# A decoder megakernel on one core: expert groups of six and two tiles, fillers placed by planned activity, last bias on VectorE, all queues in a new order

## The chip, the cores and the metric

One core of a Trainium2 chip runs the whole program. The metric is the device time of one execution in microseconds (us). TensorE (PE in the rows) multiplies matrices, VectorE (DVE) and ScalarE (ACT) work on tiles and read PSUM, GpSimd (POOL) does powers, products and indirect transfers, and SyncE (SP) starts the other transfers.

## The reference

The input x is 16 sequences of 64 tokens of 128 features. Six residual steps follow each other: an attention with ternary weights and quantised inputs (called A below), a cross attention to a context (B), a mixture of eight experts with top 2 routing, a linear attention (D), a match of every token against 64 text rows, and a feed-forward with a gridded GELU.

```python
x = x + L0_attn(layernorm(x))             # A
x = x + L0_xattn(ctx, ctx, layernorm(x))  # B
# experts: each token goes to 2 of 8 experts
h = silu(einsum('th,ehf->etf', x, w1)) * einsum('th,ehf->etf', x, w3)
out = einsum('etf,efh,te->th', h, w2, w)
x = x + L1_attn(layernorm(x))             # D
x = x + text[argmax(sim(x, text))]        # match
h = float2fix(pwlin_gelu(float2fix(x @ w1 + b1)))
x = x + float2fix(h @ w2 + b2)            # last
```

## The kernel before

The 1024 tokens are 8 tiles of 128 rows. An attention on one tile is a job, as A3 or D7. A job is a chain of stages over four engines: `stats`, `rstd` (POOL), `front`, `xT`, `xTin` (ACT), `proj`, `take` (ACT), `scores`, `shift` (DVE), for A and B also `maxT`, `qadd`, `again` and `exps` (a second pass of scores less their maximum), then `values`, `norm`, `yT`, `yTin`, `out` and `update`. Stages named `xT`, `proj`, `scores`, `again`, `values`, `yT`, `out` run on TensorE.

The experts work on groups of tiles. When the B jobs of a group are done, each tile is normalised (`pnorm`), its router logits are made (`pT`, `logits`), VectorE picks the two experts (`route`), TensorE counts the places (`rank`), VectorE makes addresses (`slots`, `table`, `home`), and POOL scatters each tile twice to HBM (`scat`, line 624, one indirect DMA of 64 KB each). Then come units of 128 rows of one expert. A group of n tiles has (2n*128 + 8*127)//128 units, whatever the router chose. SP loads weights (`W`, 768 KB, four buffers) and rows (`X`, 64 KB) of a unit and stores its result (`Y`, 64 KB). TensorE turns the rows (`xgT`, line 714), makes two halves `gu` (line 698, 8 recorded matmuls each), and `down` (line 707, 8 recorded matmuls); ACT (`uo`), DVE (`gate`) and POOL (`h`, line 602) work between `gu` and `down`. `W` of unit u waits for `down` of unit u-4. When all units of a group are stored, POOL gathers two rows for each token (`gath`, line 634) and DVE combines them (`comb`). Only then can the D jobs of those tiles start.

The end is four stages p, each for two tiles: `gstats`, `gnorm`, `gT`, `sim`, `best`, `pickT`, `got`, `gadd`, `zpow`, `znorm`, `zT` (the match), then `zh0`/`zh1`, `ha`, `nodes`, `gelu`, `blend`, `zout` (lines 983 and 985) and `finish` (the feed-forward). The stages share the tile `xz`: `gnorm` of p waits for `zT` of p-1.

The order on every engine is fixed when the program is built. `stages()` gives each stage an engine, a cost and what it waits for; `plan()` plays these costs through and takes, at each moment, the ready stage of the greatest urgency (the length of the path behind it plus a number from `URGENCY`). What runs on the chip are only the queues that come out, with semaphore waits. Where the plan has TensorE idle it puts `keep_warm`, one 384-column bf16 matmul into a bank whose contents are dead (line 992), here called a filler.

Of the kernel before, what the change touches and what calls it, by code (L numbers as in the profile page):

```python
# [67 lines left out]
URGENCY = {
    'W': 30, 'X': -10, 'Y': -56, 'add': 8, 'again': -105, 'best': -50, 'bias': -300, 'blend0': -85,
    'blend1': -30, 'clear': -3, 'comb': 30, 'down': -321, 'exps': -292, 'finish': 303, 'front': -33, 'gT': -10,  # L70
    'gTin': 30, 'gadd': -89, 'gains': -83, 'gate': -10, 'gath': -28, 'gelu0': -100, 'gelu1': -22, 'gnorm': 128,
    'got': 123, 'gu': -52, 'h': 94, 'ha0': -308, 'ha1': -300, 'home': -15, 'kept': -33, 'keyd': 30,
    'lgcopy': 312, 'logits': 326, 'maxT': 50, 'mix': -100, 'mults': -100, 'near': 30, 'nexp': -33,
    'nodes0': -10, 'nodes1': 13, 'norm': -6, 'out': 30, 'pT': -262, 'pTin': -264, 'pad': 100, 'params': -12,
    'pickT': -15, 'pickin': 38, 'pnorm': 8, 'projv': 315, 'prstd': 103, 'pstats': 10, 'qadd': 320, 'qkvout': 2,
    'rank': -6, 'rms': -297, 'rotA': 30, 'rotB': 120, 'route': -300, 'scat': -10, 'scores': 10, 'sim': 18,
    'slots': -91, 'stats': -108, 'take': -22, 'tern': -38, 'text': 46, 'textin': -128, 'tk': -103, 'tkin': -30,
    'tn': 77, 'tnT': -10, 'tnin': 97, 'tnorm': -10, 'tnorm2': -30, 'tp0': 30, 'tp1': 10, 'tpin0': -10,
    'tpin1': 10, 'tsum': -30, 'turn': 42, 'tv': 3, 'tvin': -30, 'uo': 7, 'update': -10, 'values': -113,
    'xT': 309, 'xTin': 300, 'xgT': -10, 'xgTin': -183, 'yTin': 2, 'yq': -47, 'ysave': -100, 'zT': 100,  # L80
    'zTin': -80, 'zexp': 22, 'znorm': -100, 'zout': 10, 'zpow': -13,}
# [169 lines left out]
def plan():  # L251
# [34 lines left out]
    while events:  # L286
        now = min(e[0] for e in events)
        for event in sorted(e for e in events if e[0] == now):
            events.remove(event)
            s = event[2]  # L290
            if not s:
                continue
            for filler in empties.get(s, ()):
                for bank in banks(filler):
                    full[bank] -= 1
                    freed[bank] = now
            for f in followers.get(s, ()):
                missing[f] -= 1
                if not missing[f]:
                    ready[st[f][0]].append(f)  # L300
        for e in engines:
# [1 line left out]
            if e == "tensor" and not can and free_at[e] <= now and any(ev[2] for ev in events):
                if now < fill_at:
                    if (fill_at, 1, ()) not in events:
                        events.append((fill_at, 1, ()))
                    continue
                rested = [(freed.get(name, 0.0), k) for k, name in enumerate(SPARE) if not full.get(name)]
                if not rested or min(rested)[0] > now - REST:
                    continue  # L310
                order[e].append(("keep_warm", min(rested)[1]))
                free_at[e] = now + WARM
                fill_at = now + PACE
                events.append((free_at[e], 1, ()))
# [1440 lines left out]
```

How the kernel before makes its waits and increments, by code:

```python
            def clear(_):  # L539
                sp.wait_ge(presets, PRESETS)
                sp.wait_ge(dma_param, 16)
                for g in range(NGRP):
                    sp.dma_start(d["xg"][g].rearrange("(p c r) n -> p c (r n)", p=P, c=2 * max(SIZE)),
                                 zeros[:, :].unsqueeze(1).to_broadcast([P, 2 * max(SIZE), 512])).then_inc(cleared, 16)
# [1 line left out]
            def weights_in(u):  # L547
                g, j = UNIT[u]
                sp.wait_ge(C["tab_ready"], g + 1)
                if u >= WB:
                    sp.wait_ge(C["down_mm"], u - WB + 1)
                row = sp.value_load(tab[g][0:1, 0, j:j + 1], min_val=0, max_val=(E - 1) * P)
                sp.dma_start(wbuf[:, u % WB, :], d["w"][bass.ds(row, P), :]).then_inc(w_loaded[u % WB], 16)
# [1 line left out]
            def rows_in(u):  # L555
                g, j = UNIT[u]
                sp.wait_ge(C["tab_ready"], g + 1)
                sp.wait_ge(scattered[g], 16 * 2 * SIZE[g])
                if u >= WB:
                    sp.wait_ge(C["xgT_mm"], u - WB + 1)
                row = sp.value_load(tab[g][0:1, 1, j:j + 1], min_val=0, max_val=E * REGION - P)
                sp.dma_start(xg[:, u % WB, :], d["xg"][g][bass.ds(row, P), :]).then_inc(xg_loaded[u % WB], 16)
# [1 line left out]
            def rows_out(u):  # L564
                g, j = UNIT[u]
                sp.wait_ge(C["y_saved"], u + 1)
                sp.dma_start(d["yg"][g][j * P:j * P + P, :], ys[:, u % WB, :]).then_inc(y_stored[u % WB], 16)
```

## Time and profile before

| | before |
|---|---|
| median of 3 runs | 376.45 us (375.62 to 376.56) |
| the profiled execution | 373.39 us |
| its span, first to last instruction | 371.8 us |
| TensorE busy | 331.7 us, 89% |
| VectorE, ScalarE, GpSimd busy | 236.8, 160.6, 140.3 us |
| mean granted TensorE clock | 0.945 |
| moved by DMA | 38.51 MB, mean 104 GB/s |
| fillers | 275 of 4923 recorded matmuls |

A share is an average over very different stretches: attention with hardly a transfer, experts with the DMA engines near full, and an end of short dependent steps. So the time has to be read by stretch. PEclk is the granted clock in parts of 2.4 GHz; 0.5 is the lower level, 1.2 GHz. A matmul's recorded time is a latency, so matmuls in a row are timed by the distance of their starts.

### The profile page before, as it was taken

Reading aid. Unit: us, or ns where it says so; the run is one execution under the profiler, and the core shown is the slowest. Engines: PE = TensorE matmul, PEld = TensorE weight load, DVE = VectorE, ACT = ScalarE, POOL = GpSimd, SP = SyncE. Lnnn points to the kernel's source line nnn. Section 1 sums busy time; section 2 is a strip of 40 time slices with the busy share of each in tenths; the row PEclk is TensorE's granted clock in tenths of the full one; section 3 lists DMA queues with packets and bytes.
Section 4 is the critical chain, followed back from the end, with each engine's and each line's share of the span. In section 5 each row is a group of like instructions: output and inputs, shape, how many; then the busy total and the mean of one; then the engine's idle time right before and its main releaser. Section 6 shows DMA issues by size and latency. Waiting matters only on the chain.

```text
span 371.8 us, 12672 instructions
## 1 busy us (share of the span) xinstructions
PE 331.7 (89%) x4923; PEld 262.3 (71%) x4923; DVE 236.8 (64%) x774; ACT 160.6 (43%) x466; POOL 140.3 (38%) x173
## 2 busy tenths in 40 slices
PE   0788999999999999999989888999996899977857
PEld 0335766877776778899788877999984679754535
DVE  4787755658778755256862126756679676887781
ACT  1475463523542135344545454744455065605040
POOL 5069511114283615033694367722352730110000
PEclk9999999969989889999999999999999699989895
DMA  8760000000000923605978799644300100000000
GB/s 273 281 260 2 4 2 4 4 2 4 3 4 18 330 100 103 206 9 168 294 212 255 237 307 302 218 135 158 100 15 16 53 13 5 2 0 17 0 15 14
DMA packets 19724, 38.51 MB, mean 104 GB/s; under 512 B 2129, under 2 KB 13009, under 8 KB 19538
## 3 DMA queue, kind: packets, MB, share of 16 engines
q1 hardware_dynamic: 17458, 34.62, 28.7%
q0 software_dynamic: 1024, 2.10, 1.7%
q10 hardware_dynamic: 1184, 0.99, 0.8%
q8 instruction: 39, 0.64, 0.7%
q14 instruction: 19, 0.16, 0.1%
HBM read 29.98 MB, written 7.73 MB: 101 GB/s over the span
## 4 chain that ended last, share of the span: by engine, by line
PE 63%; issue 8%; DMA 7%; DVE 6%; POOL 4%; ACT 2%; SPq 2%; POOLq 0%; ACTq 0%
PE Op L879 12%; PE FU L698 7%; PE FU L820 5%; PE Sp L806 4%; PE FU L992 4%; PE Mp L983 3%; PE AC L707 2%; PE Qp L752 2%; PE Sp L820 2%; POOL hh L602 2%; DMA yr<-yg,home 2%; PE Mp L849 2%; DMA wbuf<-in_w 1%; PE Sp L992 1%; DMA yg<-ys 1%
## 5 line engine op out<-in xcount | busy, mean ns | idle before, releaser
L596 POOL TENSOR_TENSOR rstd<-powed,minus_half 128x1 f32<-128x1 f32 (+1 forms) x36 | 22.4, 622 | 120.2 <-DVE powed L1208 94.3
L698 PE MATMUL FU<-xgT,wbuf 128*128 128x128 f32 x480 | 62.1, 277 | 4.3 <-DMA wbuf<-in_w 3.5
L698 PEld LDWEIGHTS FU<-xgT,wbuf 128*128 128x128 f32 x480 | 57.8, 192 | 7.6 <-DMA wbuf<-in_w 5.3
L602 POOL TENSOR_TENSOR hh<-hh,uu 128x256 f32<-128x256 f32 x60 | 43.2, 730 | 44.8 <-DVE hh L1533 41.3
L1533 DVE SCALAR_TENSOR_TENSOR hh<-th,FU 128x256 f32<-128x256 f32 x60 | 24.7, 420 | 37.4 <-ACT uu L1009 33.9
L1019 ACT ACTIVATE th<-FU 128x256 f32<-128x256 f32 x60 | 23.1, 385 | 44.6 <-PE FU L698 43.9
L992 PE MATMUL FU<-causal_b,identb 128*128 128x384 bf16 x149 | 36.5, 362 | 0.0
L707 PE MATMUL AC<-wbuf,hh 128*128 128x128 f32 x240 | 31.9, 276 | 2.0 <-POOL hh L602 2.0
L596 POOL TENSOR_TENSOR rms<-rms,minus_half 128x20 f32<-128x20 f32 x8 | 28.5, 3570 | 11.3 <-DVE rms L1303 11.3
L707 PEld LDWEIGHTS AC<-wbuf,hh 128*128 128x128 f32 x240 | 29.3, 192 | 2.8 <-issue 2.6
L1093 ACT ACTIVATE pT<-FU 128x1024 f32<-128x1024 f32 x16 | 16.5, 1031 | 33.9 <-PE FU L820 33.9
L1374 DVE TENSOR_REDUCE mpad<-Sp 128x8 f32<-128x512 f32 x32 | 20.6, 687 | 11.1 <-PE Sp L806 11.1
L1009 ACT ACTIVATE uu<-FU 128x256 f32<-128x256 f32 x60 | 22.9, 381 | 0.0
L983 PE MATMUL Mp<-params,hq 128*128 128x128 f32 x64 | 12.7, 361 | 9.5 <-DVE hq L1574 6.9
L992 PEld LDWEIGHTS FU<-causal_b,identb 128*128 128x128 bf16 x149 | 15.6, 108 | 7.3 <-issue 2.1
L992 PE MATMUL Sp<-causal_b,identb 128*128 128x384 bf16 x80 | 20.0, 349 | 0.0
L634 POOL DMA_INDIRECT yr<-yg,home x16 | 15.8, 985 | 11.1 <-DMA yg<-ys 8.0
L624 POOL DMA_INDIRECT xg<-xall,slot x16 | 15.9, 997 | 9.9 <-DVE slot L1461 6.2
L983 PEld LDWEIGHTS Mp<-params,hq 128*128 128x128 f32 x64 | 10.9, 257 | 11.9 <-issue 11.7
L879 PEld LDWEIGHTS Op<-vtok,pT 64*64 64x64 f32 x512 | 15.7, 135 | 2.6 <-issue 1.5
L879 PEld LDWEIGHTS Op<-textv,pT 64*64 64x64 f32 x512 | 16.1, 138 | 1.7 <-issue 0.7
L879 PE MATMUL Op<-vtok,pT 64*64 64x9 f32 x512 | 16.2, 200 | 0.8 <-issue 0.6
(264 smaller groups left out, 696.6 us busy)
## 6 DMA issues: line engine op xcount, KB each, us to landing
wbuf<-in_w SPq DMA_DIRECT2D x30, 768.0 KB
xg<-zeros SPq DMA_DIRECT2D x2, 2048.0 KB, 10.3
xg<-xg SPq DMA_DIRECT2D x30, 64.0 KB, 3.3
yg<-ys SPq DMA_DIRECT2D x30, 64.0 KB, 4.4
params<-in_params SPq DMA_DIRECT2D x1, 1632.5 KB, 10.8
x<-in_x ACTq DMA_DIRECT2D x1, 512.0 KB, 4.9
text<-in_ctx SPq DMA_DIRECT2D x1, 512.0 KB, 7.4
out<-x SPq DMA_DIRECT2D x4, 128.0 KB, 1.8
```

Of the source, the lines that this page charges most:

```text
L596: return nc.gpsimd.tensor_tensor(o, base, exponent[:, 0:o.shape[1]], ALU.pow)
L602: nc.gpsimd.tensor_tensor(hh[:, u % NB, :], hh[:, u % NB, :], uu[:, u % NB, :], ALU.mult)\
L698: ins = mm(FU[:, v % 2, 256 * part + P * i:256 * part + P * i + P], wbuf[:, u % WB, c:c + P], xgT[:, u % 2, :], start=True, stop=True)
L707: ins = mm(AC[:, 0:P], hh[:, (2 * u + i // 2) % NB, P * (i % 2):P * (i % 2) + P], wbuf[:, u % WB, c:c + P], start=i == 0, stop=i == FC - 1)
L820: ins = mm(bank[o, r, at:at + 64], key(n, c)[rows, e, o], qT[rows, b, c, o], start=first, stop=True, skip_group_check=not first)
L879: ins = mm(Op[c, w * h:w * h + w], pT[c, b, h, :], v, start=True, stop=True)
L983: ins = mm(Mp[:, P * i:P * i + P], hq[:, c, P * i:P * i + P], f_w2[:, c, :], start=(c == 0), stop=False)
L992: mm(bank, identb[:, :], causal_b[:, :].unsqueeze(1).to_broadcast([P, 6, 64]), start=True, stop=True)
L1009: return nc.scalar.activation(o, i, ACT.Copy)
L1019: nc.scalar.activation(th[:, u % NB, :], FU[:, u % 2, 0:256], ACT.Tanh, scale=0.5)
L1374: ins = v.tensor_reduce(at[:, :, r, :], sc[:, 8 * r:8 * r + 8, :].rearrange("p (c e) k -> p c e k", c=2), X, ALU.max)
L1533: v.scalar_tensor_tensor(hh[:, u % NB, :], th[:, u % NB, :], 1.0, FU[:, u % 2, 0:256], ALU.add, ALU.mult)\
```

## The change

`SIZE` goes from (4, 4) to (6, 2): the first group holds tiles 0 to 5 and has 19 units instead of 15, the second holds tiles 6 and 7 and has 11. Units 0 to 29 stay 30 in all. Group 0 makes 12 scatters and 12 gathers, group 1 makes 4 and 4. The zeroed HBM area grows from 2 x 2048 KB to 2 x 3072 KB. In the last step, the bias is no longer a matmul of one row (16 recorded matmuls in all); VectorE adds it in `finish`. The planner places fillers in a pass of its own, after the order is made, only where the planned activity of TensorE in the time just before is low. `JOBS` and `URGENCY` get other numbers, and so all queues another order. TensorE's fillers fall from 275 to 212: 51 before `out` of tile 5's B job, 48 more before the first `xgT`, 6 up to the first `down`, then none before the last `down` (unit 29), and 107 behind it. Before, they were 112 up to the end of the last B job, 37 up to the last `down`, and 126 behind.

```diff
-SIZE = (4, 4)
+SIZE = (6, 2)
 JOBS = [(j[0], int(j[1])) for j in (
-    "A0 A1 A2 A4 A3 B0 B1 B2 B3 A7 B4 A5 A6 B7 B5 B6 D0 D1 D2 D3 D4 D5 D7 D6").split()]
+    "A1 A0 A2 A4 A3 B0 B1 B2 A5 B3 B4 A7 A6 B5 B6 B7 D0 D1 D2 D4 D3 D5 D7 D6").split()]
 URGENCY = {
-    'W': 30, 'X': -10, 'Y': -56, 'add': 8, 'again': -105, 'best': -50, 'bias': -300, 'blend0': -85,
+    'W': -289, 'X': -38, 'Y': 105, 'add': 30, 'again': -83, 'best': -47, 'bias': -315, 'blend0': -50,
...
-PACE = 0.42
 REST = 1.5
+SPAN, LIVELY = 3.41, 0.48
...
-        add("zout", p, "tensor", 2.1, [("blend0", p), ("blend1", p)], "Mp", [("finish", p)])
-        add("finish", p, "vector", 0.9, [("zout", p)])
+        add("zout", p, "tensor", 1.8, [("blend0", p), ("blend1", p)], "Mp", [("finish", p)])
+        add("finish", p, "vector", 1.24, [("zout", p)])
...
+def with_fillers(stages_in_order, begun, st, vacant):
+
+    row, past, at = [], [], START["tensor"]
+    for s in stages_in_order:
+        while at + WARM <= begun[s]:
+            past = [(t, c, a) for t, c, a in past if t + c > at - SPAN]
+            lively = sum(a * (t + c - max(t, at - SPAN)) / c for t, c, a in past)
+            rested = [(f, SPARE.index(name)) for name, spells in vacant.items() for f, e in spells if f <= at - REST and e >= at + WARM]
+            if lively > LIVELY * SPAN or not rested:
+                at += 0.1
+                continue
+            row.append(("keep_warm", min(rested)[1]))
+            past.append((at, WARM, 0.16))
+            at += WARM
+        row.append(s)
+        past.append((begun[s], st[s][1], ACTIVITY.get(s[0], 0.0)))
+        at = begun[s] + st[s][1]
+    return row
...
                         ins = mm(Mp[:, P * i:P * i + P], hq[:, c, P * i:P * i + P], f_w2[:, c, :],
-                                 start=(c == 0), stop=False)
-                    ins = mm(Mp[:, P * i:P * i + P], ones[0:1, :], f_b2[0:1, :], start=False, stop=True)
+                                 start=(c == 0), stop=(c == FC - 1))
...
-                link(v.tensor_scalar(fo[:, :], Mp[:, 0:256], GRID256, GRID256, ALU.add, ALU.subtract))
+                link(v.tensor_tensor(fo[:, :].rearrange("p (t n) -> p t n", t=2), Mp[:, 0:256].rearrange("p (t n) -> p t n", t=2),
+                                     f_b2.unsqueeze(1).to_broadcast([P, 2, D]), ALU.add))
+                link(v.tensor_scalar(fo[:, :], fo[:, :], GRID256, GRID256, ALU.add, ALU.subtract))
```

TensorE's queue around the first expert unit, before (L714 is `xgT`, L698 `gu`; L752, L806 and L891 belong to attention jobs, L992 are fillers):

```order
L752 MATMUL Qp<-xnT,params 128x128 x2
L714 MATMUL Mp<-consts,xg 128x128
L992 MATMUL Sp<-causal_b,identb 128x384 x3
L806 MATMUL Sp<-keyT,qT 64x256 x8
L714 MATMUL Mp<-consts,xg 128x128
L698 MATMUL FU<-xgT,wbuf 128x128 x4
L891 MATMUL AC<-consts,yint 128x128
```

The same place of the changed program (L733 is `xgT`, L717 `gu`, L726 `down`, L1010 the fillers, L740 to L745 `rank` of group 1; L924 is the last B job's `out`, L931 and L950 `pT` and `logits` of tiles 6 and 7):

```order
L924 MATMUL AC<-params,yT 128x128
L1010 MATMUL Qp<-causal_b,identb 128x384 x10
L931 MATMUL Qp<-consts,xall 128x128 x2
L950 MATMUL Mp<-params,xallT 128x8 x2
L1010 MATMUL Sp<-causal_b,identb 128x384 x11
L733 MATMUL Mp<-consts,xg 128x128
L1010 MATMUL Sp<-causal_b,identb 128x384
L740 MATMUL Mp<-hot_b,before_b 128x16
L742 MATMUL Mp<-hot_b,ones_b 128x8
L745 MATMUL Mp<-hot_b,ones_b 128x8 x2
L717 MATMUL FU<-xgT,wbuf 128x128 x8
```

All A and B jobs now stand ahead of the first unit; before, four of the sixteen jobs were unfinished there, and their work stood between the first units. From the first `down` to `gu` 52 the changed queue is `gu`, `gu`, `down`, `xgT` over and over, with nothing else.

POOL's queue between the B jobs and the units, before (L624 scatters, L596 powers, L602 is `h`):

```order
L624 DMA xg<-xall,slot 4096x128 x8
L596 TENSOR_TENSOR rstd<-powed,minus_half 128x1
L615 TENSOR_TENSOR x<-x,params 128x128
L596 TENSOR_TENSOR rstd<-powed,minus_half 128x1
L615 TENSOR_TENSOR x<-x,params 128x128
L602 TENSOR_TENSOR hh<-hh,uu 128x256 x2
```

and in the changed program (L643 scatters, L615 powers, L621 is `h`):

```order
L643 DMA xg<-xall,slot 6144x128 x12
L615 TENSOR_TENSOR rstd<-powed,minus_half 128x2
L643 DMA xg<-xall,slot 6144x128 x4
L621 TENSOR_TENSOR hh<-hh,uu 128x256 x43
L653 DMA yr<-yg,home 128x128
```

The first `h` now stands behind twelve scatters of group 0 and behind all four of group 1; before, behind eight of group 0 alone.

TensorE's queue behind the last `down`, before (the last row shown is `pickT` of p = 1; `gT` of p = 0 was long done):

```order
L912 MATMUL Qp<-consts,xz 128x128 x2
L707 MATMUL AC<-wbuf,hh 128x128 x4
L946 MATMUL Mp<-tnormT,xzT 64x64 x4
L992 MATMUL Sp<-causal_b,identb 128x384 x9
L912 MATMUL Qp<-consts,pick 128x128 x2
```

and in the changed program, where `gT` of p = 0 follows the last `down`, and work of D2, D4, D3 and D5 stands behind it:

```order
L726 MATMUL AC<-wbuf,hh 128x128 x4
L931 MATMUL Qp<-consts,xz 128x128 x2
L924 MATMUL Op<-params,yT 128x128
L779 MATMUL Mp<-xnT,params 128x128
L780 MATMUL Mp<-params,xnT 128x144
L771 MATMUL Qp<-xnT,params 128x128 x2
L773 MATMUL Qp<-xnT,params 128x128
L898 MATMUL Op<-vn,pT 64x8 x32
```

So all four stages p lie behind the last unit now, where before the first was past its match, and only two D jobs wait for the last gathers instead of four.

## Rows read from the trace of the kernel before

**Rows 1.** The page: busy time, share, instructions of each engine.

```profile
PE 331.7 (89%) x4923; PEld 262.3 (71%) x4923; DVE 236.8 (64%) x774; ACT 160.6 (43%) x466; POOL 140.3 (38%) x173
```

**Rows 2.** Windows: stretch, its length, busy (count) per engine, PEclk, DMA share, GB/s.

```profile
0.00:167.06 167.06, 152.71 (x2791) 111.02 (x2792) 107.74 (x411) 71.14 (x195) 63.23 (x70) 0.95 0.26 89
167.06:281.05 113.99, 105.33 (x1286) 97.78 (x1287) 64.22 (x193) 57.49 (x196) 59.93 (x81) 1.00 0.62 196
281.05:338.29 57.24, 50.15 (x732) 38.29 (x733) 44.07 (x127) 23.67 (x59) 16.48 (x22) 0.91 0.06 17
338.29:371.80 33.51, 23.49 (x120) 15.20 (x118) 20.81 (x46) 8.34 (x17) 0.69 (x1) 0.80 0.03 9
```

**Rows 3.** Windows of line 992 alone, the fillers: PE and PEld.

```profile
0.00:167.06 167.06, 29.02 (x112) 12.17 (x112) 0.95 0.26 89
167.06:281.05 113.99, 9.72 (x37) 3.87 (x37) 1.00 0.62 196
```

**Rows 4.** Timeline of PE, jobs and first units: start, us, what.

```profile
115.09 0.18 PE L721 MATMUL Mp<-hot_b,before_b 128*128 128x32 bf16 x1
...
133.89 0.48 PE L714 MATMUL Mp<-consts,xg 128*128 128x128 f32 x1
...
141.41 1.06 PE L707 MATMUL AC<-wbuf,hh 128*128 128x128 f32 x8
...
147.79 1.09 PE L806 MATMUL Sp<-keyT,qT 64*64 64x256 f32 x16
...
149.19 1.16 PE L820 MATMUL FU<-qT,keyT 64*64 64x64 f32 x64
...
156.67 2.04 PE L879 MATMUL Op<-textv,pT 64*64 64x9 f32 x64
158.64 0.49 PE L905 MATMUL AC<-params,yT 128*128 128x128 f32 x2
```

**Rows 5.** Timeline of DVE: B3's update, then first and last of route.

```profile
100.77 0.29 DVE L1419 TENSOR_TENSOR x<-x,AC 128x128 f32<-128x128 f32 x1 [0.20 <-PE AC L905]
...
111.14 0.18 DVE L1431 TENSOR_REDUCE thr<-base 128x4 f32<-128x32 f32 x1
...
113.59 0.19 DVE L1449 TENSOR_TENSOR hot_b<-hot 128x32 bf16<-128x32 f32 x1
```

**Rows 6.** Timeline of POOL: first and last of eight scatters.

```profile
116.78 1.18 POOL L624 DMA_INDIRECT xg<-xall,slot  x1 [5.38 <-DVE slot L1461]
...
125.94 0.96 POOL L624 DMA_INDIRECT xg<-xall,slot  x1 [0.30 <-issue]
```

**Rows 7.** Timeline of SP: a W, then (left out) X and Y, the next W.

```profile
211.87 0.34 SPq L553 DMA_DIRECT2D wbuf<-in_w  x1
...
214.67 0.34 SPq L553 DMA_DIRECT2D wbuf<-in_w  x1
```

**Rows 8.** Timeline of PE: two downs of one unit's distance.

```profile
193.44 1.06 PE L707 MATMUL AC<-wbuf,hh 128*128 128x128 f32 x8
...
196.23 1.06 PE L707 MATMUL AC<-wbuf,hh 128*128 128x128 f32 x8
```

**Rows 9.** Windows as above: eight units, four W alone, jobs at the lower clock.

```profile
201.09:231.57 30.48, 25.74 (x212) 23.94 (x213) 9.59 (x27) 14.66 (x50) 17.39 (x23) 1.00 0.87 278
128.00:131.00 3.00, 2.83 (x76) 2.24 (x69) 1.87 (x9) 1.28 (x4) 0.42 (x1) 0.74 1.01 414
73.70:82.20 8.50, 8.50 (x157) 6.90 (x157) 3.81 (x18) 2.20 (x5) 1.47 (x3) 0.60 0.01 2
```

**Rows 10.** Timeline of PE: zT of p = 2 and 3, last fillers, last bias.

```profile
335.16 0.44 PE L912 MATMUL Qp<-consts,xz 128*128 128x128 f32 x2
...
351.67 0.38 PE L912 MATMUL Qp<-consts,xz 128*128 128x128 f32 x2
...
354.58 3.58 PE L992 MATMUL FU<-causal_b,identb 128*128 128x384 bf16 x21
...
367.64 0.79 PE L985 MATMUL Mp<-params,ones 1*128 1x128 f32 x2
```

More of the change, by code:

```diff
@@ L72 @@
[L72 to L76, printed above, removed]
@@ new lines @@
+    'blend1': -50, 'clear': -300, 'comb': -18, 'down': -309, 'exps': -10, 'finish': 4, 'front': -48, 'gT': 30,
+    'gTin': -105, 'gadd': 80, 'gains': 300, 'gate': 300, 'gath': -100, 'gelu0': 3, 'gnorm': -30, 'got': 369,
+    'gpow': -300, 'gstats': -100, 'gu': -100, 'h': 331, 'ha0': -8, 'ha1': -31, 'home': 109, 'kept': 30,
+    'keyd': -30, 'lgcopy': 24, 'logits': -39, 'maxT': 128, 'mix': -100, 'mults': -300, 'near': -20,
+    'nexp': -300, 'nodes0': 30, 'nodes1': 122, 'norm': 7, 'out': 323, 'pT': 10, 'pTin': -10, 'pad': 100,
@@ new lines @@
+    'params': 27, 'pickT': -100, 'projv': 308, 'prstd': -108, 'pstats': -11, 'qadd': 92, 'qkvout': 300,
+    'rank': 10, 'rms': -38, 'rotA': 10, 'rotB': 13, 'rotM': -100, 'route': -100, 'rstd': -10, 'scat': 30,
+    'scores': 73, 'shift': 10, 'sim': 33, 'slots': -280, 'stats': -102, 'table': 297, 'take': 100, 'tern': -52,
+    'text': 21, 'tk': -52, 'tn': -30, 'tnT': -131, 'tnin': -280, 'tnorm': -10, 'tnorm2': 100, 'tp0': 30,
+    'tp1': 10, 'tpin0': -10, 'tpin1': 10, 'tsum': -300, 'turn': 337, 'tv': -78, 'tvin': -300, 'uo': -41,
@@ L82 @@
+    'update': 7, 'values': -65, 'xT': 280, 'xTin': -10, 'xgT': 26, 'xgTin': 22, 'yT': 10, 'yTin': 58, 'yq': 305,
+    'ysave': -348, 'zT': -10, 'zTin': 2, 'zexp': 20, 'zh0': -50, 'zh1': 260, 'znorm': 141, 'zout': -300,
+    'zpow': 128,}
 LANDING = {'scat': 3.0, 'gath': 2.8, 'W': 5.0, 'X': 2.6, 'Y': 4.2}
@@ L85 @@
 WARM = 0.18
-PACE = 0.42
 REST = 1.5
+SPAN, LIVELY = 3.41, 0.48
+ACTIVITY = {
+    "xT": 0.11, "turn": 0.32, "projv": 0.45, "maxT": 0.21, "values": 0.12, "yT": 0.11, "tk": 0.85, "tv": 0.43, "text": 0.21,
+    "tnT": 0.21, "pT": 0.21, "logits": 0.03, "xgT": 0.11, "gu": 0.85, "down": 0.85, "gT": 0.21, "sim": 0.21, "pickT": 0.21,
+    "got": 0.43, "zT": 0.21, "zh0": 0.85, "zh1": 0.85, "zout": 1.7, "scores": 0.9, "again": 0.95, "proj": 0.35, "out": 0.16}
 SPARE = ("FU0", "FU1", "AC", "Qp", "Mp", "Op", "Sp")
@@ L275, in plan @@
     free_at = dict(START)
-    full, freed, empties, fill_at, table = {}, {}, {}, 0.0, 0
+    full, empties, table, begun = {}, {}, 0, {}
+    vacant = {name: [[0.0, 1e9]] for name in SPARE}
     waiting = set(turn_of.values()) | set(turn_of)
@@ L295, in plan @@
                     full[bank] -= 1
-                    freed[bank] = now
+                    if not full[bank] and bank in vacant:
+                        vacant[bank].append([now, 1e9])
             for f in followers.get(s, ()):
@@ L302, in plan @@
             can = [s for s in ready[e] if not any(full.get(k) for k in banks(s)) and turn_of.get(s) not in waiting] if free_at[e] <= now else []
[L303 to L314, printed above, removed]
             if can:
```

11 lines of the change are left out of this document (4 added, 7 removed).

## The prediction

> **What bounds the kernel now.** The page comes first: TensorE is busy 89% of the span, no other engine over 64% [rows 1]. That is not yet a bound, since 275 of its matmuls are fillers. So the next view is the table of windows, cut where the work changes [rows 2], and the same windows for the fillers' line [rows 3]. Up to the end of the last B job (167.06 us), TensorE is busy 152.7 us with 112 fillers in it. A filler in a row takes 0.163 us: 21 of them start at 354.58 and end 3.58 us later, less one latency of 0.33 [rows 10]. So the fillers are 18.3 us there, and TensorE, or what feeds it, is the bound: it has almost no idle time after the first 30 us, and where a filler stands it either fills a wait or delays real work by its length. From 167.06 to 281.05 us (last `down`) TensorE is busy 105.3 of 114.0 with 37 fillers, at DMA share 0.62: units and four D jobs, a dense stretch. In the last 90.75 us (the third and fourth of [rows 2]) TensorE is busy with fillers, the real chain runs through VectorE (64.9 busy) and short steps on all engines. The reader should see three regimes: TensorE-bound attention, units paced by TensorE, SP and weights together, and a serial end.
>
> **The change, stretch by stretch.** I cut the changed program at the same kinds of places and work out each length.
>
> *Start to `out` of B5 (job 13).* Before takes 167.06 to finish all B jobs. Off come 112 fillers (18.3) and the expert work inside: 14 blocks of `gu` or `down` and 7 `xgT`. One unit is 2.79 us from `down` to `down` when nothing waits [rows 8], so a block is 0.89 and an `xgT` 0.11: 13.3 in all. Off also comes what now lies behind `out` of B5, two B jobs and two router steps. A B job is scores 1.09, again 1.16, values 2.04, out 0.49 [rows 4] and about 0.9 for its small matmuls: 5.7, so 12.0. On come the 51 fillers that stay: 8.3. That is 131.8 if no wait shows up where the other 61 fillers (9.9) stood. If all of it does, 141.7. Since the queue is reordered to have other work there, I take a fifth: +2.0, so **133.8**. The clock I leave as it was.
>
> *`out` of B5 to `rank` of group 0.* All six tiles must be routed before anything of an expert starts. The chain is update, normalisation, `pT`, logits, `route` (2.65 from 111.14 to 113.78, [rows 5]), and ahead of the logits copy on VectorE stand B6's front and shift, which wait for its projection and scores: with 0.3 to 0.4 for each small step and 1.1 and 1.3 for scores and shift I get 8.6. Before, B3's update to `rank` was 14.3 (100.77 to 115.09, [rows 4, 5]), with TensorE full of other jobs; that is the upper end. **8.6.**
>
> *`rank` to the end of the first `down`.* Before: 115.09 to 141.41 + 0.9 = 27.2, hidden under attention jobs [rows 4]. Scatters follow each other at 1.26 us ((125.94 - 116.78)/7 = 1.31 with a slow first, [rows 6]); four more cost 5.0. Then POOL's order matters: the first `h` is behind group 1's four scatters, which need `rank` of group 1, and that stands behind the first `xgT` on TensorE. `xgT` comes at 18.8 + 5.0 + 0.8 (slots now wait for a shift) = 24.6 after `rank`; then rank and slots of group 1 (1.7), four scatters (5.0), two `h` (1.6), `down` (1.0): **33.9**. What hides it: remaining TensorE work there is two halves of B jobs and four `gu`, about 13 us. So some 20 us of TensorE are bare now that before were covered. This is the price of the grouping. `W` is queued early and has no part in it.
>
> *First `down` to `gu` 52.* Unit after unit with nothing between. TensorE's floor is 2.79 [rows 8]. SP's floor is 2.80: W, X and Y, and the next W at 211.87 and 214.67 [rows 7]. The transfers: a unit moves 0.917 MB, and eight units with their gathers had 278 GB/s at share 0.87 [rows 9], so 320 GB/s at full share and 2.87 us a unit. These eight units took 30.48 us, 3.81 each [rows 9], but with waits of SP out of step and gathers between. Three floors of 2.8 to 2.9 beside each other do not add up to 2.87; I take 3.05, nearest to the floors because the new SP queue repeats W, Y, X regularly. The first two units run on loaded weights (6.1), then 22 units: 6.1 + 22 x 3.05 = **73.2**. Bounds: 2.79 gives 67.5, 3.81 gives 89.9.
>
> The Trainium skill (DMA: Bandwidth & Descriptors, § Specifications) gives about 358 GB/s as the HBM limit of a core. By it a unit would be 2.56 us, under TensorE's 2.79, and this stretch 67.5 instead of 73.2. The rows do not bear the figure out either way: with four W alone in flight 414 GB/s moved [rows 9], with X, Y and gathers among them 278 at share 0.87. I go by the rows.
>
> *`gu` 52 to the last `down`.* 8 `gu`, 6 `down`, 2 `xgT`: 12.7. Beside them stand 3.6 D jobs. Before, the like stretch is `gu` 44, where [rows 9] end (231.57), to the last `down` at 281.05: 49.5 us, with 25 blocks and 6 `xgT` of units in it (23.0), a match of about 4 and some fillers, so four D jobs took about 22, or 5.5 each. 12.7 + 3.6 x 5.5 = **32.7**.
>
> *Last `down` to the end.* Before: 90.75 us [rows 2]. Now `gT` of p = 0 starts right there, and through `xz` the four stages p form one chain. Up to `gT` of p = 3, before needed 57.24, with VectorE busy 44.1. Now VectorE has there: 44.1, plus match of p = 0 and start of p = 1 (6.4), plus remainders of D4, D3, D5 (7.7), less two D jobs that are done (9.0), plus the longer `finish` (0.9) = 50. It is 88% full, and I find the same 57 when I walk its new order. Behind it, before took 33.51; the bias matmuls go (2 x 0.72 of the last p at this clock, [rows 10]), one blend moves out of the way of `gadd` (1.2 of it helps), the new add costs 0.45: 31.3. **88.3.** The cover of the bias matmuls in p = 0 to 2 is VectorE's own work, so they gain nothing there.
>
> Sum: 133.8 + 8.6 + 33.9 + 73.2 + 32.7 + 88.3 = **370.5**, against 371.8 before, 1.3 less. The profiled execution was 373.39 in time, the median of the runs shown is 376.45; I take the difference off the median: about **375**.
>
> The zeroing of HBM grows by 2 MB. It runs in the first 50 us beside nothing that waits for it, since scatters start after 100 us: 0. `rank` has 12 matmuls instead of 8, under 0.1.
>
> **The rivals.** A measurement of this kernel can tell a change from about 0.3%, 1.1 us.
>
> *Dense units at TensorE's floor and attention that closes up.* 2.79 instead of 3.05 saves 5.7, no returned waits 2.0: 367. For it: the floors of SP and TensorE are equal and nothing else is in the queues. Against: the eight units of [rows 9].
>
> *The last stretch is shorter.* Only two D tiles remain behind the last gathers. If the walk through VectorE overstates and the chain through `xz` alone counts (13.4 a match, from 338.29 to 351.67, and 3.1 to the next `gT`, from 335.16 to 338.29 [rows 2, 10], three times, and 31.3), it is 81, and the whole about 368. Against: VectorE is nearly full.
>
> *Weights fall behind: slower.* W of a unit waits for `down` four units before, in a dense row that is twice the unit's time for issue and landing. If one more transfer in flight makes it land later, the pace is 3.4 to 3.81, and the stretch 7.7 to 16.7 longer: 383 to 392. It decides at 3.16 a unit, where the gain of 1.3 and 1.1 more are eaten. The eight units of [rows 9] speak for it.
>
> *The filler time comes back: slower.* All 9.9 us become waits, or the clock falls more often because TensorE has fewer fillers: +8, 383. The clock fell before in 73.7 to 82.2 us to a mean of 0.60 with TensorE busy 8.50 of 8.50 us and fillers in the row [rows 9], so idle time alone is not what does it, and fillers did not prevent it. The Trainium skill (TensorE: Matmul & The Clock Gate, § Why this matters for your kernels) ties the fall to idle gaps between bursts; by that the bare 20 us before the units would start them at 1.2 GHz and, lasting as in [rows 9], cost some 4 us, while the closed-up attention would be safe. The row contradicts it for the attention.
>
> *The change does nothing.* If all gains and prices cancel, 376.
>
> **How the numbers follow.** The forecast as worked out, 371 to 379, 0.42. Units at the floor or closed-up attention 0.18, shorter end 0.15, weights behind 0.13, fillers' time back 0.12. Of the forecast's own 0.42, 0.19 lie under 375.3, 0.10 within 0.3%, 0.13 above. Faster: 0.19 + 0.18 + 0.15 = 0.52; same 0.10; slower 0.13 + 0.25 = 0.38. For 8 in 10 the range goes to 364 below (both gains together) and 384 above.
>
> **What would show it.** The first `xgT` at about 167 us and a hole before it with TensorE on fillers and idle; the first `h` behind the sixteenth scatter; `down` to `down` 3.0 to 3.1 us for some 22 units, with short waits on wbuf; last `down` at 282; the end 88 long with VectorE over 80% busy up to `gT` of p = 3. Wrong would be: `out` of B5 outside 128 to 140, a unit's pace outside 2.9 to 3.2, an end under 84.

## The result and the profile after

The changed kernel took 380.39 us in the median of 8 runs (378.15 to 383.98), the kernel before 376.38 (375.13 to 378.47): a ratio of 1.0133, 95% interval 1.009 to 1.0177. Medians, here and below, are over all runs; ratios and their intervals leave out runs over 1.5% above the fastest of the same kernel. The changed kernel is slower by 1.3%; forecast was about 375, slightly faster. The profiled execution took 380.45 us with a span of 378.8, against the 370.5 of the sum. Its table of busy times, to be set beside [rows 1]:

```profile
PE 323.1 (85%) x4844; PEld 258.9 (68%) x4844; DVE 233.2 (62%) x778; ACT 161.9 (43%) x466; POOL 140.7 (37%) x173
```

TensorE is 8.6 us less busy and the span is 7 us longer, so the loss is idle time and slower matmuls, not more work. The windows, cut at the places of the prediction's sum (end of B5's `out`, end of the first `down`, end of the last, `gT` of p = 3), as [rows 2]:

```profile
0.00:138.06 138.06, 120.80 (x2293) 85.69 (x2293) 87.98 (x333) 59.00 (x153) 46.20 (x49) 0.92 0.21 72
138.06:180.80 42.74, 32.41 (x436) 23.14 (x436) 27.55 (x121) 8.77 (x25) 20.04 (x23) 0.91 0.33 113
180.80:287.30 106.50, 101.09 (x1214) 97.68 (x1213) 47.07 (x130) 60.90 (x211) 60.30 (x83) 0.98 0.72 233
287.30:345.65 58.35, 49.59 (x799) 38.54 (x798) 49.25 (x149) 24.85 (x62) 13.09 (x17) 0.97 0.04 12
345.65:378.80 33.15, 19.17 (x108) 13.89 (x107) 21.33 (x48) 8.41 (x17) 1.11 (x1) 0.89 0.03 9
```

| term of the sum | forecast | measured | |
|---|---|---|---|
| start to `out` of B5 | 133.8 | 138.1 | +4.3 |
| to `rank` of group 0 | 8.6 | 10.5 | +1.9 |
| to the end of the first `down` | 33.9 | 32.3 | -1.6 |
| to `gu` 52 | 73.2 | 74.5 | +1.3 |
| to the end of the last `down` | 32.7 | 32.0 | -0.7 |
| to the end | 88.3 | 91.5 | +3.2 |

The first window's clock is 0.92, where the kernel before had 0.95 over its own first window [rows 2]. Three stretches up to `rank` of group 0 have a low clock, while TensorE is busy nearly all the time:

```profile
78.00:88.50 10.50, 10.50 (x170) 8.37 (x167) 5.87 (x26) 4.09 (x10) 3.71 (x7) 0.52 0.01 3
103.00:108.50 5.50, 5.37 (x130) 5.08 (x133) 3.46 (x15) 1.72 (x7) 4.51 (x3) 0.70 0.01 3
128.90:144.50 15.60, 14.31 (x115) 9.56 (x115) 7.08 (x30) 2.77 (x9) 2.65 (x5) 0.56 0.01 2
```

By the clocks of these rows the lower level (0.5) held for some 27 us of the first 148.5; by that of [rows 2], for some 17 of the first 167 before. Both are estimates: twice what the clock lacks to 1, times the length.

The bare hole, on TensorE's timeline (L740 `rank`, L1010 fillers, L931 `pT`, L733 `xgT`, L726 `down`):

```profile
148.52 0.20 PE L740 MATMUL Mp<-hot_b,before_b 128*128 128x48 bf16 x1 [0.81 <-DVE qT L1400]
...
162.57 2.12 PE L1010 MATMUL Qp<-causal_b,identb 128*128 128x384 bf16 x10
167.47 0.44 PE L931 MATMUL Qp<-consts,xall 128*128 128x128 f32 x2 [2.78 <-DVE xall L1229]
...
170.70 0.27 PE L733 MATMUL Mp<-consts,xg 128*128 128x128 f32 x1
...
179.77 1.13 PE L726 MATMUL AC<-wbuf,hh 128*128 128x128 f32 x8 [1.13 <-POOL hh L621]
```

Of the 23 distances from `down` to `down` in the dense units, 17 are 2.78 to 3.01 us, five lie between 3.46 and 4.01 and one is 5.36. The one long wait for a W costs 1.90 us itself and about as much again by the lower clock behind it: two distances of 5.36 and 4.01 us where two of 2.79 would be 3.8 less:

```profile
226.65 2.50 PE L717 MATMUL FU<-xgT,wbuf 128*128 128x128 f32 x16 [1.90 <-DMA wbuf<-in_w]
228.94 1.91 PE L726 MATMUL AC<-wbuf,hh 128*128 128x128 f32 x8
```

At the end (L1002 `zout`, L931 `zT`), `zout` of p = 2 and 3 each stand on the path after an idle wait and run at the lower clock; those of p = 0 and 1, at the upper, take 1.95 and 2.02 us. In the trace of before, `zout` of p = 2 is at the upper clock (348.36 us) and the last at the lower, as here. VectorE writes the second half of `xz` for `zT` of p = 3 by 357.50, and `zT` starts at 360.07 since it is queued behind `zout` of p = 2. VectorE's row, then TensorE's:

```profile
356.90 0.60 DVE L1229 TENSOR_SCALAR xz<-x,mv,rstd 128x128 f32<-128x128 f32 x2
```

```profile
357.13 3.15 PE L1002 MATMUL Mp<-params,hq 128*128 128x128 f32 x16 [2.65 <-DVE hq L1592]
360.07 0.63 PE L931 MATMUL Qp<-consts,xz 128*128 128x128 f32 x2
...
371.60 3.58 PE L1002 MATMUL Mp<-params,hq 128*128 128x128 f32 x16 [4.79 <-DVE hq L1592]
```

### The profile page after: what moved, and what is told of

Its sections match the earlier page's. It is cut to its first block, busy times and chain, and to the rows that moved or that the text cites. A ratio compares the mean times of both kernels' runs of the same rounds, so it can differ in the third digit from the quotient of the medians.

```text
span 378.8 us, 12522 instructions
## 1 busy us (share of the span) xinstructions
PE 323.1 (85%) x4844; PEld 258.9 (68%) x4844; DVE 233.2 (62%) x778; ACT 161.9 (43%) x466; POOL 140.7 (37%) x173
## 4 chain that ended last, share of the span: by engine, by line
PE 24%; DVE 14%; DMA 7%; issue 5%; SPq 2%; POOL 2%; ACT 1%; DVEq 0%; POOLq 0%; ACTq 0%
PE FU L717 7%; DMA wbuf<-in_w 5%; PE AC L726 4%; PE Op L898 3%; PE Mp L1002 2%; PE Sp L839 2%; DVE keyT L1590 2%; DVE keyT L1591 1%; DMA yr<-yg,home 1%; DVE keyT L1589 1%; DMA yg<-ys 1%; PE Qp L991 1%; DVE pT L1384 1%; DVE keyT L1578 1%; DVE stats L1220 1%
## 5 line engine op out<-in xcount | busy, mean ns | idle before, releaser
L717 PE MATMUL FU<-xgT,wbuf 128*128 128x128 f32 x480 | 61.4, 280 | 4.1 <-DMA wbuf<-in_w 3.3
L615 POOL TENSOR_TENSOR rstd<-powed,minus_half 128x1 f32<-128x1 f32 (+1 forms) x36 | 22.3, 620 | 107.4 <-DVE powed L1226 97.9
L717 PEld LDWEIGHTS FU<-xgT,wbuf 128*128 128x128 f32 x480 | 57.2, 194 | 6.1 <-DMA wbuf<-in_w 4.6
L621 POOL TENSOR_TENSOR hh<-hh,uu 128x256 f32<-128x256 f32 x60 | 43.3, 729 | 36.0 <-DVE hh L1551 35.9
L615 POOL TENSOR_TENSOR rms<-rms,minus_half 128x20 f32<-128x20 f32 x8 | 28.3, 3541 | 23.6 <-DVE rms L1321 23.6
L1037 ACT ACTIVATE th<-FU 128x256 f32<-128x256 f32 x60 | 23.0, 383 | 30.7 <-PE FU L717 30.5
L726 PE MATMUL AC<-wbuf,hh 128*128 128x128 f32 x240 | 32.8, 281 | 2.5 <-POOL hh L621 2.5
L726 PEld LDWEIGHTS AC<-wbuf,hh 128*128 128x128 f32 x240 | 30.1, 197 | 2.9 <-issue 2.9
L1010 PE MATMUL FU<-causal_b,identb 128*128 128x384 bf16 x146 | 30.8, 341 | 0.0
L1111 ACT ACTIVATE pT<-FU 128x1024 f32<-128x1024 f32 x16 | 16.4, 1023 | 26.4 <-PE FU L839 26.3
L643 POOL DMA_INDIRECT xg<-xall,slot x16 | 15.6, 976 | 21.1 <-DVE slot L1479 16.8
L898 PEld LDWEIGHTS Op<-textv,pT 64*64 64x64 f32 x512 | 18.7, 157 | 4.2 <-issue 3.7
L898 PE MATMUL Op<-textv,pT 64*64 64x9 f32 x512 | 19.4, 214 | 2.1 <-issue 1.9
L1010 PEld LDWEIGHTS FU<-causal_b,identb 128*128 128x128 bf16 x146 | 14.9, 104 | 7.4 <-issue 1.2
L1002 PE MATMUL Mp<-params,hq 128*128 128x128 f32 x64 | 10.7, 337 | 8.2 <-DVE hq L1592 8.2
L898 PEld LDWEIGHTS Op<-vn,pT 64*64 64x64 f32 x512 | 15.8, 137 | 2.3 <-DVE x L1437 1.4
L898 PE MATMUL Op<-vn,pT 64*64 64x8 f32 x512 | 16.5, 201 | 0.7 <-DVE x L1437 0.7
L898 PE MATMUL Op<-vtok,pT 64*64 64x9 f32 x512 | 16.4, 201 | 0.5 <-issue 0.4
## 6 DMA issues: line engine op xcount, KB each, us to landing
params<-in_params SPq DMA_DIRECT2D x1, 1632.5 KB, 10.5
```

The costliest lines, as they stand in the source:

```text
L615: return nc.gpsimd.tensor_tensor(o, base, exponent[:, 0:o.shape[1]], ALU.pow)
L621: nc.gpsimd.tensor_tensor(hh[:, u % NB, :], hh[:, u % NB, :], uu[:, u % NB, :], ALU.mult)\
L717: ins = mm(FU[:, v % 2, 256 * part + P * i:256 * part + P * i + P], wbuf[:, u % WB, c:c + P], xgT[:, u % 2, :], start=True, stop=True)
L726: ins = mm(AC[:, 0:P], hh[:, (2 * u + i // 2) % NB, P * (i % 2):P * (i % 2) + P], wbuf[:, u % WB, c:c + P], start=i == 0, stop=i == FC - 1)
L898: ins = mm(Op[c, w * h:w * h + w], pT[c, b, h, :], v, start=True, stop=True)
L1010: mm(bank, identb[:, :], causal_b[:, :].unsqueeze(1).to_broadcast([P, 6, 64]), start=True, stop=True)
```

## The experiments

Two theories. **Order:** the loss is the bare hole of the grouping and the later end. **Clock:** fewer fillers, elsewhere, let TensorE's clock fall. The runs were made in five groups, each on a chip of its own: `b_bias`, `b_both`, `a_paced`, `a_none`; `a_again`, `a_wlate`, `b_wlate`, `a_split`; `a_ref`, `a_half`, `a_more`, `bb_split`; `a_scatlate`, `a_more_split`, `bb_more`; `a_ref2`, `a_scatlate2`, `bb_more2`. The kernel before had medians of 378 to 387 there, and 376 beside the result; ratios are to before on the same chip, clocks are means over a kernel's runs. A name with a is an edit of the changed kernel, with b or bb one of the kernel before.

**One part alone in the kernel before.** Bias on VectorE with all queues as they were (`b_bias`); with the new filler pass besides (`b_both`).

```diff
-                                 start=(c == 0), stop=False)
-                    ins = mm(Mp[:, P * i:P * i + P], ones[0:1, :], f_b2[0:1, :], start=False, stop=True)
+                                 start=(c == 0), stop=(c == FC - 1))
...
+    real = [s for s in order["tensor"] if s in st]
+    order["tensor"] = with_fillers(real, begun, st, vacant)
```

> The kernel before with one edit: the bias of the last step is added by VectorE, all queues as before. My theory (the bias counts only in the last of the four stages): 2 x 0.72 us of one-row matmuls go, 0.45 us of VectorE comes, 1.0 us less than before, about 375.4. Rival (the gain is hidden or eaten by VectorE in the first three stages): 376.4 to 377.

> The kernel before with the bias on VectorE and the new filler pass, the order of the real work on all queues as before: 190 fillers instead of 275 (80 instead of 108 ahead of the first down, 3 instead of 41 up to the last, 107 instead of 126 behind). Theory 1 (the change lost by its grouping and order, fillers are neutral): within 1 us of the run with the bias alone, about 375. Theory 2 (fewer fillers cost clock or stand in the wrong places): 3 to 4 us more than the bias alone, 378 to 379, with a mean granted clock below 0.94.

`b_bias`: 376.61 against 384.92, ratio 0.980 (0.972 to 0.988), clock 0.949 against 0.934. `b_both`: 387.74, ratio 1.009 (1.002 to 1.017), clock 0.923. So the new filler pass alone, with 190 fillers instead of 275, took 11 us and 0.026 of the clock: theory 2 of `b_both`, three times as large. Where it loses, one profile of each tells. It reaches `rank` of group 0 at 113.9 us, `b_bias` at 113.8, both at clock 0.97 up to there; to the first `down` it loses 3.9 us, and 7.9 more from the first `down` to the last (`b_bias` first):

```profile
146.84:286.02 139.18, 130.10 (x1806) 119.52 (x1805) 75.34 (x221) 68.35 (x228) 67.08 (x91) 1.00 0.57 181
150.78:297.85 147.07, 131.53 (x1769) 121.88 (x1767) 76.52 (x221) 68.61 (x227) 67.04 (x91) 0.95 0.53 171
```

So the new pass costs clock and time in this order too, but not ahead of `rank`, where the changed kernel lost most.

That the bias gives 8 us and not 1 is explained in part. From the last `down` to the end, the two profiles with the bias matmuls in this order take 91.8 (before) and 92.3 us (`b_wlate`, below), the two without them and with nothing else changed there but fillers 87.9 and 88.3: about 4 us. The last stage p alone is 1.6 shorter than before's (31.96 against the 33.51 of [rows 2]). Where the other 4 us come from stays open.

**Fillers in the changed kernel.** The old rule (`a_paced`), none (`a_none`), a higher limit (`a_more`).

```diff
-    order["tensor"] = with_fillers(order["tensor"], begun, st, vacant)   # a_none
...
-SPAN, LIVELY = 3.41, 0.48
+SPAN, LIVELY = 3.41, 0.75
```

> The changed kernel with the old rule for fillers (one for each 0.42 us of planned idle time): 242 fillers instead of 212, 117 ahead of the first down instead of 105, 19 instead of none up to the last. Theory 1 (fillers neutral): 380, within 1 us of the changed kernel. Theory 2 (the new pass costs clock): 377 to 378 with a granted clock above that of the changed kernel.

> The changed kernel without any filler. Theory 1 (the clock needs them only in the thin stretches): the end doubles its 10.5 us of real matmuls behind gT of p = 3 and about as much before it in part, and the first units start at the lower clock: 388 to 395, mean clock under 0.85. Rival (fillers delay real work as much as they keep the clock): 378 to 382.

> The changed kernel with the limit of planned activity at 0.75 instead of 0.48, so 394 fillers instead of 212: 105 ahead of out of B5 where there are 51 (the kernel before has 110), 194 behind the last down instead of 107. Theory 1 (the attention stretch is late because the clock falls more often without the fillers): granted clock up by 0.02 to 0.04, rank of group 0 at 143 to 146 instead of 148 to 151, the whole 3 to 8 us less. Theory 2 (fillers stand in the way of real work): the clock rises less than the 183 fillers of 0.163 us each cost, 3 to 10 us more.

`a_paced`: 399.26, 1.042 (1.036 to 1.048), on a chip without the changed kernel beside it, so it decides nothing by its time; its profile reaches `rank` of group 0 at 145.0 us, within the spread of the changed kernel's own (below). `a_none`: 419.42 against 384.92, clock 0.818. `a_more`: 395.63, 1.028 (1.021 to 1.035), clock 0.944, beside the changed kernel (`a_ref`) with 407.61, 1.073 (1.054 to 1.092), clock 0.898. 182 more fillers made it 12 us faster. In windows from the start to `rank` of group 0, `a_ref` first, then `a_more`:

```profile
0.00:146.42 146.42, 127.77 (x2352) 89.18 (x2352) 94.64 (x360) 60.93 (x160) 47.73 (x52) 0.92 0.19 68
```

```profile
0.00:140.58 140.58, 128.99 (x2419) 89.59 (x2420) 94.73 (x360) 61.20 (x160) 47.74 (x52) 0.99 0.20 71
```

All 13 profiles with this order lie near one line, about 1 us for 0.01 of clock up to `rank`: 158.1 at 0.85 (`a_none`), 151.2 at 0.89 (`a_split`), 148.5 at 0.91 (the result's), 145.4 at 0.94 (`a_ref2`), 142.2 and 140.6 at 0.99 (`a_more_split`, `a_more`). Nine of them have the very same queue of TensorE up to there, and still spread from 0.89 to 0.94 and from 145.1 to 151.2 us; the two with 54 more fillers ahead of `out` of B5 lie outside that spread, each ahead of the other profiles of this order on its chip (140.6 against 146.4 and 150.2, 142.2 against 149.5).

**The changed kernel again, W later, `zout` in two.** `a_wlate` and `b_wlate` move the second to fourth W behind the first X, since the profiles of the first group had shown TensorE idle by issue behind the four W.

```diff
+        for u in (3, 2, 1):
+            sp_row.remove(("W", u))
+            sp_row.insert(sp_row.index(("X", u)), ("W", u))
```

> The changed kernel itself, once more, beside the kernel before on the chip of this call. The old ratio was 1.013. Theory 1 (the loss is the bare stretch of the grouping and the later end, fixed by the queues): the ratio stays at 1.010 to 1.018. Theory 2 (the size of the loss comes from the clock and from TensorE waiting for instructions while the four first W are in flight, which differ by run and chip): the ratio moves, to under 1.00 or over 1.02, and with it the mean granted clock and the idle time put down to issue.

> The changed kernel as it is, only to have it on the same chip as the other runs of this call. By the two ratios seen so far, 1.013 or 1.054 to the kernel before: near the second where its profile shows TensorE waiting by issue while the twelve scatters of group 0 run, near the first where it doesn't.

> The changed kernel with the second, third and fourth W each moved in SP's queue from ahead of the first X to just ahead of their own X. Theory 1 (nothing but the four transfers keeps TensorE from its instructions there; in the profile with paced fillers 8.2 us of idle time by issue lie in the 20 us after the first W): 5 to 9 us less than the changed kernel wherever that shows such gaps, 0 to 1 where it doesn't, the second unit not later, since its W is issued about 168 us and used about 176. Theory 2 (the gaps have another cause, or the weights now come late for the first units): same or 2 to 6 us more.

> The kernel before with the same edit on SP's queue alone. Theory 1: where before has gaps by issue behind its four W (6.0 us in the profile with the bias alone), they go, but the three later W now run under the jobs and first units that stand right behind, so some come back: 2 to 6 us less. Theory 2: no change, or 2 to 4 us more because W of the second unit is 3 us from its use.

`a_again`: 408.48 against 381.30, ratio 1.054 (1.046 to 1.062), and `a_ref`, shown above, 1.073: on these chips the change costs four to five times as much. What came on top is mostly one stall: of the 22 us by which the profile of `a_again` is longer than the result's, 14.8 lie between `rank` of group 0 and the first `down`, and 4.6 between the last `down` and `gT` of p = 3. TensorE's timeline of `a_ref2`, the same program on a fourth such chip (L898 `values`, L839 `again` of B6 and B7):

```profile
148.05 2.08 PE L898 MATMUL Op<-textv,pT 64*64 64x9 f32 x58 [0.17 <-ACT pT L1111]
150.56 0.26 PE L898 MATMUL Op<-textv,pT 64*64 64x9 f32 x2 [0.43 <-issue]
...
156.34 0.47 PE L839 MATMUL FU<-qT,keyT 64*64 64x64 f32 x2 [0.95 <-issue]
...
162.75 0.26 PE L839 MATMUL FU<-qT,keyT 64*64 64x64 f32 x1 [1.03 <-issue]
...
164.88 1.57 PE L839 MATMUL FU<-qT,keyT 64*64 64x64 f32 x45 [0.44 <-issue]
```

A few matmuls, then half to one microsecond of nothing, for 14 us, with no semaphore in the way. The result's own profile has one gap there, of 1.07 us at 156.90, ahead of the `values` of B7. `a_scatlate2`, below, has 0.79 us at that same place with no scatter near, so this one is no part of the stall. `a_wlate`: 408.23, and 9.2 us of gaps by issue in the 20 us behind its first W, now alone, where `a_again` has 9.7 (the brackets of the timeline's rows summed): so the three later weights are not the cause, and in `a_again` the gaps begin at 154.70, ahead of the first W at 155.43. `b_wlate`: 385.07, ratio 1.007 (1.000 to 1.013); nothing gained there either.

The order of before is not free of the stall. From `rank` of group 0 to the first `down`, it takes 26.3 us in the trace of before and 29.3 in `bb_more`, but 33.0 to 37.1 in its five profiles on the four chips where the changed kernel stalls, a part of it by a lower clock. `b_bias` has three gaps there, 4.33, 0.45 and 1.05 us by issue, from 120.4 to 127.8. So these ratios count only what the stall costs the changed kernel more, and some of what before differs by chip is the stall too.

The cut of `zout` into two parts (`a_split`):

```diff
+                for c0 in (0, 2) if two_parts else (0,):
+                    if c0:
+                        for _ in range(8):
+                            keep_warm(0)
+                        pe.wait_ge(Z["hq_ready"][1], p + 1)
```

> The changed kernel with zout of p = 2 and 3 in two parts: the eight matmuls on the first half of hq as soon as blend0 is done, eight fillers, then the other eight. Theory (zout of p = 2 and 3 stands bare on the path at the lower clock, 3.15 and 3.58 us, and zT of p = 3 waits behind the first of them): 3.0 us less at the lower clock, 4.5 less if the fillers bring it to the upper one. Rival (VectorE is the chain there and takes up what TensorE gives): under 1 us less.

`a_split`: 404.15 beside 408.48, 4.3 less. From `gT` of p = 3 to the end it takes 29.8 us where `a_again` takes 34.4. The edit does two things, since the eight fillers are part of it: `a_more`, with `zout` whole and more fillers, takes 30.7 there, `a_more_split` 29.1. So most of the 4.6 us seems to be the clock, and some 1.6 the cut. Its last `zT` starts 1.0 us behind the start of the second part (L1009), in `a_again` 2.8 behind that of the whole:

```profile
381.44 1.46 PE L1018 MATMUL FU<-causal_b,identb 128*128 128x384 bf16 x8
383.27 1.16 PE L1009 MATMUL Mp<-params,hq 128*128 128x128 f32 x8 [0.36 <-DVE hq L1600]
384.26 0.38 PE L931 MATMUL Qp<-consts,xz 128*128 128x128 f32 x2
```

**Who stalls TensorE.** The twelve scatters run in that very stretch. `a_half` leaves out the second scatter of each tile of group 0, so those rows stay zero, and lets SP wait for six instead of twelve. `a_scatlate`, and again `a_scatlate2`, moves all twelve behind the router's last power.

```diff
+                if g == 0 and k:
+                    return
...
+        at = pool_row.index(("prstd", 3)) + 1
+        pool_row[at:at] = early
```

> The changed kernel with the second scatter of each tile of group 0 left out, so that those rows stay zero: six scatters instead of twelve, nothing else. Theory 1 (TensorE's stall belongs to the scatters: while they run it gets its instructions slowly): the stall ends with the sixth scatter, half as long, and the first unit comes 7.6 us sooner for the missing issues; where the reference shows the stall, the first down comes 8 to 15 us sooner, where it doesn't, 7 to 8. Theory 2 (the stall has nothing to do with the scatters): it stays 13 to 14 us long, and the first down comes 0 to 3 us sooner since TensorE is late anyway.

> The changed kernel with the twelve scatters of group 0 moved in POOL's queue from ahead of the last power of the router (prstd of tiles 6 and 7) to just behind it. So TensorE does the rest of B6 and B7 (again, values, out) before any scatter runs. Theory 1 (the scatters keep TensorE's instructions away): no gaps by issue between rank and the last out, that part takes 12 to 14 us as in the first profile of the changed kernel instead of 27 to 30, power at rank + 15 instead of + 32, first xgT at rank + 33 to 36, so about where it stood (rank + 37): 0 to 4 us less in all. Theory 2 (the gaps belong to this place of TensorE's program, whatever POOL does): the gaps stay, the scatters come behind them, and the first xgT is at rank + 50 or later, 13 us more.

> The changed kernel, one look beside the next kernel. It tells only whether this chip shows the stall: TensorE's last values of B6 start 6 us behind rank without it and 20 us or more with it.

> The changed kernel with the scatters of group 0 behind the router's last power, again. If the look before shows the stall: by theory 1 (the scatters cause it) no gaps by issue here, the router's last power at rank + 15 to 17 and the first xgT at rank + 34 to 37; by theory 2 (the place causes it) gaps as in the look before and the first xgT at rank + 48 or later. If that look shows no stall, nothing is told.

`a_half`: 400.13 beside 407.61; `rank` to the first `down` 37.6 us where `a_ref` has 45.7. POOL's last scatter, and TensorE's last gap:

```profile
159.13 0.96 POOL L645 DMA_INDIRECT xg<-xall,slot  x1 [0.30 <-issue]
```

```profile
161.18 1.99 PE L841 MATMUL FU<-qT,keyT 64*64 64x64 f32 x60 [0.45 <-issue]
```

The stall ends 1.1 us behind the sixth scatter; in `a_ref2` it ends 2.0 behind the twelfth (161.92 + 0.96). From the first gap to the end of the last it lasts 6.3 us, in `a_ref2` 14.8. `a_scatlate` (395.20, 1.044, 1.033 to 1.054) told nothing on this: on its chip `a_more_split`, with the scatters in place, has no stall either. On the chip of `a_ref2`, `a_scatlate2` has its scatters from 165.88 on, and the same two stages before them (L904, L845) run through:

```profile
152.29 2.04 PE L904 MATMUL Op<-textv,pT 64*64 64x9 f32 x64 [0.17 <-ACT pT L1117]
154.26 1.15 PE L1016 MATMUL AC<-causal_b,identb 128*128 128x384 bf16 x6
155.34 1.16 PE L845 MATMUL FU<-qT,keyT 64*64 64x64 f32 x64
...
184.93 0.47 PE L739 MATMUL Mp<-consts,xg 128*128 128x128 f32 x1 [15.16 <-DMA xg<-xg]
...
185.91 3.76 PE L723 MATMUL FU<-xgT,wbuf 128*128 128x128 f32 x16
```

The stall is gone, as theory 1 had it, in one profile of each of the two kernels. The first `xgT` stands at `rank` + 35.3 where `a_ref2` has 36.6, as expected; but TensorE then sat idle for 15 us and does its first two `gu` at the lower clock (3.76 us, 2.02 in the result's timeline at 172.12).

**Both kernels mended.** Bias, split and, in two of them, the limit of 0.75, on the old queues and on the new.

> The kernel before with two edits, the bias on VectorE and zout of p = 2 and 3 in two parts with eight fillers between: a candidate to beat both kernels. The bias alone had 0.980 of before, and in the changed kernel the split took the last stage from gT of p = 3 to the end from 33 or 34 to 29.8 us. Expected 3 to 4 us less than the bias alone, a ratio of 0.970 to 0.975. Rival (VectorE is fuller there in this order): the ratio stays at 0.98.

> The kernel before with the bias on VectorE, zout of p = 2 and 3 in two parts, and the new filler pass with its limit at 0.75: 363 fillers instead of 275 (183 instead of 132 up to the first down, 15 instead of 41 up to the last, 197 instead of 126 behind). If the clock decides, as in the changed kernel where 394 instead of 212 fillers brought it from 0.898 to 0.944 and the time from 406.4 to 394.8: granted clock 0.96 to 0.97 and a ratio of 0.96 to 0.975. If the order before has no idle time left for them, they delay real work: 0.98 to 1.00.

> The changed kernel with the limit at 0.75 and zout of p = 2 and 3 in two parts, 410 fillers in all: with more fillers alone it had 1.028 of before, the split takes another 2 to 4 us off the last 31: ratio 1.015 to 1.025. It does not reach the kernel before where the scatters stall TensorE for 14 us; where they don't, it would be at 0.97 to 0.985.

> The kernel before with the bias on VectorE, zout in two parts and 363 fillers, once more on another chip. It had 0.980 there with the clock at 0.978. Expected 0.965 to 0.985: more gain where the clock of before is lower.

`bb_split`: 378.91, 0.982 (0.972 to 0.992), no more than the bias alone and not the 0.970 to 0.975 expected. `bb_more`: 369.48, 0.980 (0.974 to 0.987), clock 0.978; `bb_more2`, on another chip, 374.95, 0.984 (0.975 to 0.993), clock 0.977. None of the three is ahead of `b_bias` by its ratio (0.980 at clock 0.949): in the order of before the extra fillers raised the clock, and the gain expected of it (0.96 to 0.975) did not come. `a_more_split` beside `bb_more`, on the chip without a stall: 374.93, 0.983 (0.977 to 0.989), clock 0.980. So `bb_more` beats the kernel before on two chips, and on the second it is far ahead of the one run there of the changed kernel (401.88). On the new queues the same mending reaches the same clock and stays 5.5 us behind in the medians, but by the ratios only 1.1, and their intervals overlap: that it is slower is not shown. Profile against profile it is 366.1 and 372.9 us at 0.991 and 0.986. The windows of each from `rank` of group 0 to its first `down`, `bb_more` first:

```profile
112.66:141.96 29.30, 27.22 (x458) 20.11 (x454) 18.70 (x77) 8.88 (x25) 11.67 (x15) 0.88 0.41 144
```

```profile
142.17:175.16 32.99, 27.37 (x394) 19.65 (x395) 20.07 (x93) 6.69 (x18) 17.96 (x20) 0.95 0.43 145
```

## Why the prediction was wrong, step by step

**Start to `rank`, the step that failed.** "The clock I leave as it was." It fell from 0.95 to 0.92, and 6.1 us were missed in the first two terms. The three profiles of this order at 0.94, nearest to the clock that the sum assumed, reach `rank` at 145.0 to 145.4 where the sum says 142.4; the result's, at 0.91, at 148.5. So a good 3 of the 6.1 us are the clock. The other 2.6 to 3.0 are missing at the assumed clock too: the counts of removed fillers, blocks and jobs, or the fifth for returned waits, were too hopeful together, and no run tells which. Only at 0.99, with 54 more fillers, is 142.4 reached (140.6 and 142.2). The error of the clock was to count a filler as 0.163 us and nothing else. I took the clock's fall at 73.7 to 82.2 with TensorE fully busy [rows 9] as a sign that fillers don't matter; one such stretch showed that they do not always help. With 51 fillers instead of 112 there, such stretches cover 27 us instead of 17, by the estimate above; of this the spread between runs of one program, 0.89 to 0.94, may be a part.

The Trainium skill (TensorE: Matmul & The Clock Gate, § Why this matters for your kernels) ties the fall to idle gaps between bursts. `a_none` agrees in direction (0.818 of clock, with idle time in place of fillers); the three rows above, busy 30.18 of 31.60 us at 0.52 to 0.70, do not follow from that rule.

**The hole.** 33.9 forecast, 32.3 measured, first `down` behind sixteen scatters: right. "Some 20 us of TensorE are bare" is right too, as the fillers and idle time from 159 to 171 show. That it would be harmless apart from its length was only true of the result's chip: on four of the five later ones the twelve scatters also stopped TensorE's own jobs for 14 us.

**Units, D jobs.** 3.05 a unit forecast, 3.13 in the mean of 23, and 74.5 us against 73.2 for the stretch. The mean is not a steady pace, though: 17 units run near TensorE's floor of 2.79, the others take 3.46 and more, three of them with a wait for a W. Beyond these waits the weights did not fall behind. 32.0 against 32.7 for the D jobs; the terms of that sum, 12.7 and 3.6 times 5.5, give 32.5.

**The end.** 88.3 forecast, 91.5 measured. VectorE's walk to `gT` of p = 3 was 1.4 short. The other 1.85 lies between that `gT` and `zT` of p = 3: 14.4 us, where before took 13.4 [rows 2, 10] and the forecast took 1.2 off. There `zout` of p = 2 takes 3.15 us at the lower clock and `zT` stands behind it. From `zT` to the end it is 18.7 us against 20.1, a little more off than forecast. So here too the clock was left as it was; `a_split`, which cuts `zout` and adds fillers, took 4.6 us off the last stage.

**The bias.** Forecast at 1.0 for the last p and nothing in the others; between the last `down` and the end, the profiles above show about 4 us, at a better clock.

**The rivals.** The one that came true is "the filler time comes back", in its second form: the clock falls more often. It was priced at 383, with 0.12. Whether some filler time came back as waits too is open, by the 2.6 to 3.0 us above. The grouping and order, taken at equal clock and without the stall, seem to cost between 1 us (by the ratios) and 7 (by the two profiles), where the sum had the whole change 1.3 us ahead; that part is the least certain. No run has the old grouping in a new order or the new grouping alone, so the two are not told apart.
